# Local attention in tiles of 32 queries and 64 keys, with two heads to a transpose

## The reference

```
WINDOW = 32;  HEADS = 16;  DIM_HEAD = 64;  QK_SCALE = 8
def local_attention(q, k, v):          # b, h, n, d
    # queries in windows of 32; each window sees its own 32 keys and the 32 before
    mask = (it < jb) | (it > jb + w) | (jb == -1)
    sim = einsum('bhwie,bhwje->bhwij', bq, bk2) * QK_SCALE     # 32 x 64 per window
    attn = softmax(where(mask, -max, sim))
    out = einsum('bhwij,bhwje->bhwie', attn, bv2)
def attn_layer(x, Wqkv, qs, ksc, Wo):
    q, k, v = split(x @ Wqkv);  q = l2norm(q) * qs;  k = l2norm(k) * ksc
    q, k = rotary with position scales (q, k)
    return local_attention(q, k, v) @ Wo
for i in range(6):
    x = attn_layer(shift_tokens(x), ...) + x
    x = ffn_layer(shift_tokens(x), ...) + x      # layer norm, 128 -> 2 x 341, a * gelu(gate), -> 128
```

## Time and profile before

| | |
|---|---|
| time, median of 3 runs | 3379.95 us (3378.38 to 3385.42) |
| the profiled execution's own time | 3382.95 us |
| its span | 3380.9 us |
| TensorE matmuls busy | 2973.2 us (88%), 29755 instructions |
| DVE, ACT, POOL busy | 71%, 55%, 38% |
| chain that ended last | TensorE 76%, DVE 16%, everything else 8% |
| DMA | 127.31 MB, 13.1% of 16 engines on the main queue |

### The profile page before, as it was taken

One profiled execution on the slowest core, in us unless ns is written; L12 is line 12 of the kernel. 1 busy time (PEld: TensorE's weight loads), 2 busy tenths in 40 slices (PEclk: granted clock), 3 DMA queues, 4 the chain that ended last, 5 costly groups with the idle time before them and its releaser, 6 DMA issues.

```text
span 3380.9 us, 74255 instructions
## 1 busy us (share of the span) xinstructions
PE 2973.2 (88%) x29755; PEld 1802.7 (53%) x29812; DVE 2400.9 (71%) x3960; ACT 1874.8 (55%) x4990; POOL 1290.9 (38%) x851
## 2 busy tenths in 40 slices
PE   4669858475979799999599999999999999999997
PEld 3544546352334333333376666666666666666665
DVE  4950289537940677776688888888888888888885
ACT  4221331135422266666377777777777777777774
POOL 0010000100000111111377766766776676676663
PEclk7579855597989799999799999999999999999999
DMA  2000000000000100000221212122121221211111
GB/s 100 3 1 0 36 3 3 1 0 0 0 0 0 61 23 23 24 22 16 99 56 48 52 46 79 48 59 73 45 59 49 79 53 45 79 48 47 42 44 40
DMA packets 38966, 127.31 MB, mean 38 GB/s; under 512 B 8480, under 2 KB 10784, under 8 KB 36736
## 3 DMA queue, kind: packets, MB, share of 16 engines
q1 hardware_dynamic: 38656, 122.96, 13.1%
HBM read 43.57 MB, written 5.44 MB: 14 GB/s over the span
## 4 chain that ended last, share of the span: by engine, by line
PE 76%; DVE 16%; DVEq 2%; ACT 2%; issue 2%; DMA 1%; POOLq 1%; ACTq 0%; SPq 0%; POOL 0%
PE ps L1481 15%; PE ps L648 7%; PE ps L1533 6%; PE ps L1523 5%; PE ps L1499 5%; PE ps L1541 5%; PE ps L1514 5%; DVE arena L972 4%; PE ps L1076 4%; PE ps L1104 4%; PE ps L1554 4%; PE ps L1091 3%; PE ps L1506 2%; PE ps L1560 2%; PE ps L200 1%
## 5 line engine op out<-in xcount | busy, mean ns | idle before, releaser
L1481 PE MATMUL ps<-arena 128*128 128x512 f32 x1152 | 555.3, 604 | 15.8 <-ACTq L1763 14.4
L1828 ACT ACTIVATE arena<-ps,arena 128x96 f32<-128x96 f32 x1536 | 497.9, 350 | 81.4 <-DVE arena L2017 81.3
L2094 POOL TENSOR_TENSOR arena<-arena 128x1024 f32<-128x1024 f32 x190 | 448.7, 2362 | 113.5 <-DVE arena L1908 113.5
L2100 POOL TENSOR_TENSOR arena<-arena 128x2048 f32<-128x2048 f32 x95 | 344.2, 3623 | 199.0 <-ACT arena L1770 193.6
L1241 DVE TENSOR_REDUCE arena<-ps 128x1 f32<-128x512 f32 x512 | 329.5, 686 | 77.2 <-PE ps L1076 72.0
L1203 ACT ACTIVATE arena<-ps 128x1024 f32<-128x1024 f32 x256 | 262.2, 1024 | 178.6 <-PE ps L1091 169.9
L2089 POOL TENSOR_TENSOR arena<-arena 128x768 f32<-128x768 f32 x192 | 282.7, 1472 | 131.4 <-DVE arena L1943 131.4
L1828 ACT ACTIVATION_READ_ACCUMULATOR arena<-ps,arena 128x1 f32 x1536 | 332.6, 217 | 0.0
L1903 DVE TENSOR_TENSOR arena<-ps,arena 128x1024 f32<-128x1024 f32 x192 | 235.1, 1225 | 121.4 <-PE ps L1481 107.8
L1481 PEld LDWEIGHTS ps<-arena 128*128 128x128 f32 x1152 | 197.6, 191 | 169.9 <-issue 157.6
L191 POOL TENSOR_SCALAR rstd<-mv 128x4 f32<-128x4 f32 x32 | 8.1, 252 | 718.7 <-DVE mv L178 718.7
(11 more groups left out here) (285 smaller groups left out, 5422.8 us busy)
## 6 DMA issues: line engine op xcount, KB each, us to landing
arena<-pack_l SPq DMA_DIRECT2D x48, 384.0 KB, 4.1
arena<-grow SPq DMA_DIRECT2D x48, 384.0 KB, 4.0
arena<-in_deep SPq DMA_DIRECT2D x6, 2649.5 KB, 9.5
arena<-pack_l SPq DMA_DIRECT2D x48, 256.0 KB, 3.5
arena<-grow SPq DMA_DIRECT2D x48, 256.0 KB, 3.4
arena<-in_rotary SPq DMA_DIRECT2D x6, 1024.0 KB, 8.4
arena<-pack_l SPq DMA_DIRECT2D x48, 128.0 KB, 2.3
pack_tern<-in_tern SPq DMA_DIRECT2D x2, 2888.0 KB, 10.5
```

Source lines behind the costliest of these rows:

```text
L1481: last = T.matmul(m.ps[0:rows.stop - rows.start, at + half, :], f.xs[t % 2][:, rows], w.wqkv[:, j * INNER + half * BLK:j * INNER + (half + ...
L1828: last = A(f.prob[:, p, :], m.ps[:, 4 + j % 2, i * SPAN:(i + 1) * SPAN], ACT.Exp, bias=f.nmax[t % 2][:, p:p + 1], accum_out=f.rsum[t % 2][ ...
L2094: G.tensor_tensor(f.rot[t % 2][:, here], f.rot[t % 2][:, here], f.sin[:, here], ALU.add)
L2100: G.tensor_tensor(r, r, spread(f.ss[t % 2], DH), ALU.mult).then_inc(s["rotated"], 1)
```

## The change

`SPAN`, the keys of a product, goes from 96 to 64, and the queries from 64 to 32 (`WINS` = 4 windows a tile). Scores are computed for each head in 4 products of 32 queries and 64 keys; the bands have 64 columns for each head. Within a call, heads are taken in pairs (even, odd) so that exponentials write the probabilities of head 2k and 2k+1 beside each other. A transpose then takes such a pair, 128 columns, and puts the even head's keys on rows 0 to 63 and the odd head's on rows 64 to 127; `probs(j)` makes 4 of them in one bank, and `pT` is half as wide. Value products take 64 rows and 32 queries, 4 a head. For this the values must lie on the same rows as the probabilities: `vraw` is written with all even heads first and then all odd ones, and the spreading puts even heads on rows 0 to 63 and odd ones on rows 64 to 127, for each window 64 rows: 8 DMAs, and 2 for the next tile's first 32 rows. Since `probs(1)` has a bank of its own now, its wait on the copy of the first half (`p_copied`) goes.

```diff
@@ -40,7 +40,7 @@
...
 PACKS = {
-    "const": [("ident", P), ("band", 96), ("band0", 96), ("cT", 2 * LAYERS)],
+    "const": [("ident", P), ("band", 64), ("band0", 64), ("cT", 2 * LAYERS)],
     "mod": [("wmod", LAYERS * 6 * P)],
@@ -1437,11 +1437,11 @@
...
 WIN = 32
+WINS = P // WIN
 HALF = P // 2
-SPAN = WIN + HALF
+SPAN = 2 * WIN
 KEYS = WIN + P
 FRONT = WIN + 1
-ORDER = [h for half in range(2) for odd in range(2) for h in range(8 * half + odd, 8 * half + 8, 2)]
 GROUP = 4
@@ -1468,7 +1468,7 @@
...
-    return sum(2 + (u % BT != 0) for u in range(t % 2, t + 1, 2))
+    return sum(8 + 2 * (u % BT != 0) for u in range(t % 2, t + 1, 2))
@@ -1507,32 +1507,32 @@
...
         for i in range(GROUP):
-            for half in range(2):
+            for w in range(WINS):
                 for e in range(2):
-                    h = ORDER[GROUP * (j + e) + i]
-                    rows = slice(DH * e, DH * e + DH)
-                    last = T.matmul(m.ps[HALF * half:HALF * (half + 1), 4 + e, i * SPAN:(i + 1) * SPAN],
-                                    f.qT[rows, h // 2, HALF * half:HALF * (half + 1)],
-                                    f.kT[t % 2][rows, h // 2, HALF * half:HALF * half + SPAN], start=False, stop=True,
+                    k = 2 * j + i
+                    rows, queries = slice(DH * e, DH * e + DH), slice(WIN * w, WIN * (w + 1))
+                    last = T.matmul(m.ps[queries, 4 + e, i * SPAN:(i + 1) * SPAN], f.qT[rows, k, queries],
+                                    f.kT[t % 2][rows, k, WIN * w:WIN * w + SPAN], start=False, stop=True,
                                     skip_group_check=True)
-                    if i == GROUP - 1 and half == 1:
+                    if i == GROUP - 1 and w == WINS - 1:
                         last.then_inc(s["scored"], 1)
...
     def probs(j):
-        for i in range(8):
-            last = T.transpose(m.ps[0:SPAN, PROB_AT + i // 4, (i % 4) * P:(i % 4 + 1) * P], f.prob[:, 8 * j + i, :],
-                               m.ident)
+
+        for i in range(GROUP):
+            last = T.transpose(m.ps[:, PROB_AT + j, i * P:(i + 1) * P], f.flat_prob[:, 4 * j + i, :], m.ident)
         last.then_inc(s["p_made"], 1)
...
     def heads(t):
-        for i in range(QB):
-            for half in range(2):
-                col = (i % 4) * P + HALF * half
+        for n in range(QB):
+            for w in range(WINS):
                 for e in range(2):
-                    h = 2 * i + e
-                    last = T.matmul(m.ps[DH * e:DH * (e + 1), HEADS_AT + i // 4, col:col + HALF],
-                                    f.v[t % 2][0:SPAN, half, h * DH:(h + 1) * DH],
-                                    f.pT[0:SPAN, ORDER.index(h), HALF * half:HALF * (half + 1)], start=True, stop=True)
+                    i = (n + 4 * e) % QB
+                    rows, queries = slice(DH * e, DH * (e + 1)), slice(WIN * w, WIN * (w + 1))
+                    col = (i % 4) * P + WIN * w
+                    last = T.matmul(m.ps[rows, HEADS_AT + i // 4, col:col + WIN],
+                                    f.v[t % 2][rows, w, i * DH:(i + 1) * DH], f.pT[rows, i, queries],
+                                    start=True, stop=True)
         last.then_inc(s["heads"], 1)
@@ -1634,7 +1634,6 @@
...
         if behind:
-            pe.wait_ge(s["p_copied"], 2 * t - 1)
             pe.wait_ge(s["normed"], 2 * t)
@@ -1824,7 +1823,7 @@
...
             for i in range(GROUP):
-                p = GROUP * j + i
+                p = 8 * (j // 2) + 2 * i + j % 2
                 last = A(f.prob[:, p, :], m.ps[:, 4 + j % 2, i * SPAN:(i + 1) * SPAN], ACT.Exp,
@@ -1857,8 +1856,7 @@
...
         act.wait_ge(s["p_made"], 2 * t + 1)
-        A(f.pT[0:SPAN, 0:8, :], wide(PROB_AT, SPAN).rearrange("p a (i b) -> p (a i) b", b=P),
-          ACT.Copy).then_inc(s["p_copied"], 1)
+        A(f.pT[:, 0:4, :], m.ps[:, PROB_AT, :].rearrange("p (i b) -> p i b", b=P), ACT.Copy).then_inc(s["p_copied"], 1)
@@ -1880,7 +1878,8 @@
...
     for v in f.v:
-        V.memset(v[0:WIN, 0, :], 0.0)
+        for e in range(2):
+            V.memset(v[DH * e:DH * e + WIN, 0, :], 0.0)
     V.memset(f.mean, 1.0 / P)
@@ -1929,12 +1928,12 @@
...
             dve.wait_ge(s["v_spread"][(t - 1) % 2], 16 * v_moves(t - 1))
-        V.tensor_copy(f.vraw[t % 2].rearrange("p (a b) -> p a b", a=2), m.ps[:, at:at + 2, :]).then_inc(s["v_copied"], 1)
+        V.tensor_copy(f.vraw[t % 2].rearrange("p (e i d) -> p i e d", e=2, d=DH),
+                      m.ps[:, at:at + 2, :].rearrange("p a (i e d) -> p (a i) e d", e=2, d=DH)).then_inc(s["v_copied"], 1)
...
         dve.wait_ge(s["p_made"], 2 * t + 2)
-        V.tensor_copy(f.pT[0:SPAN, 8:16, :],
-                      m.ps[0:SPAN, PROB_AT:PROB_AT + 2, :].rearrange("p a (i b) -> p (a i) b", b=P))\
+        V.tensor_copy(f.pT[:, 4:8, :], m.ps[:, PROB_AT + 1, :].rearrange("p (i b) -> p i b", b=P))\
             .then_inc(s["p_copied"], 1)
@@ -2014,7 +2013,7 @@
...
             dve.wait_ge(s["scored"], 4 * t + j + 1)
-            V.tensor_reduce(f.nmax[t % 2][:, GROUP * j:GROUP * (j + 1)],
+            V.tensor_reduce(f.nmax[t % 2][:, 8 * (j // 2):8 * (j // 2) + 8].rearrange("p (i e) -> p e i", e=2)[:, j % 2, :],
                             m.ps[:, 4 + j % 2, 0:GROUP * SPAN].rearrange("p (h k) -> p h k", h=GROUP), AX, ALU.max,
@@ -2174,12 +2173,18 @@
...
         sp.wait_ge(s["v_copied"], t + 1)
-        sp.dma_start(v[t % 2][WIN:SPAN, 0, :], raw[0:HALF, :]).then_inc(s["v_spread"][t % 2], 16)
-        sp.dma_start(v[t % 2][0:SPAN, 1, :], raw[WIN:P, :]).then_inc(s["v_spread"][t % 2], 16)
+        for e in range(2):
+            here, at = slice(e * BLK, (e + 1) * BLK), DH * e
+            sp.dma_start(v[t % 2][at + WIN:at + SPAN, 0, :], raw[0:WIN, here]).then_inc(s["v_spread"][t % 2], 16)
+            for w in range(1, WINS):
+                sp.dma_start(v[t % 2][at:at + SPAN, w, :], raw[WIN * (w - 1):WIN * (w + 1), here])\
+                    .then_inc(s["v_spread"][t % 2], 16)
         if t % BT != BT - 1:
...
                 sp.wait_ge(s["heads"], t)
-            sp.dma_start(v[(t + 1) % 2][0:WIN, 0, :], raw[P - WIN:P, :]).then_inc(s["v_spread"][(t + 1) % 2], 16)
+            for e in range(2):
+                sp.dma_start(v[(t + 1) % 2][DH * e:DH * e + WIN, 0, :], raw[P - WIN:P, e * BLK:(e + 1) * BLK])\
+                    .then_inc(s["v_spread"][(t + 1) % 2], 16)
@@ -2226,9 +2231,10 @@
...
     f.sin = a.take(2 * INNER)
-    f.v = [a.take(2 * INNER).rearrange("p (a b) -> p a b", a=2) for _ in range(2)]
-    f.pT = a.take(LH * P).rearrange("p (a b) -> p a b", b=P)
-    f.prob = a.take(LH * SPAN).rearrange("p (a b) -> p a b", b=SPAN)
+    f.v = [a.take(2 * INNER).rearrange("p (a b) -> p a b", a=WINS) for _ in range(2)]
+    f.pT = a.take(QB * P).rearrange("p (a b) -> p a b", b=P)
+    prob = a.take(LH * SPAN)
+    f.prob, f.flat_prob = (prob.rearrange("p (a b) -> p a b", b=n) for n in (SPAN, 2 * SPAN))
     f.kT = [a.take(QB * KEYS).rearrange("p (a b) -> p a b", b=KEYS) for _ in range(2)]
@@ -2464,9 +2470,9 @@
...
-    i, j = np.arange(P)[:, None], np.arange(96)[None, :] - 32
-    seen = (j <= i % 64) & (j >= i % 64 - 32)
-    first = seen & ((j >= 0) | (i >= 64))
+    i, j = np.arange(P)[:, None], np.arange(2 * WIN)[None, :] - WIN
+    seen = (j <= i % WIN) & (j >= i % WIN - WIN)
+    first = seen & ((j >= 0) | (i >= WIN))
     big = np.float32(-1e30)
...

```

## The result

The changed kernel takes 3456.65 us (median of 4 runs, 3453.61 to 3458.89) against 3380.44 before: a ratio of 1.0223, 95% interval 1.0211 to 1.0236. It is slower by 76 us, 2.2%; forecast were 51 us, 1.5%. The profiled execution took 3453.61 us, its span is 3451.7.

The account below looks back on a forecast made before the run. TensorE was taken to bound the last stage; value products +1.88, scores -0.26, transposes -0.88 and bands -0.21 gave +0.53 us a visit, times 96 +51 us: 3431 us, range 3382 to 3480.

Parts of the forecast that it names:

- What bounds the kernel: Last stage, 96 visits: its time is the sum of TensorE's blocks, busy 1666.88 of 1676 us at full clock.
- The value products: Heads block: 64 rounds, each as long as loading 64 stationary columns; 3.90 us against 2.02, +1.88 us a visit.
- Rival A: Value products: the load hides, a round is 32 ns, heads costs only +0.16 us a visit; 3266 us, chance 0.12.
- Rival B: Scores and value products: each instruction costs its start, +2.58 us a visit; 3628 us, chance 0.04.
- The scores: Score blocks, two calls a visit: middle taken between -0.21 and -0.05 us a call, -0.13; -0.26 us a visit.
- the ideal of 8 rounds: Score block: eight products at once, limited by streaming; 0.61 us against 0.82, -0.21 us a call.
- Transposes and bands: Transposes of probabilities, 4 a call instead of 8: -0.88 us a visit; bands, 256 columns instead of 384: -0.21.
- What lies beside: Shorter DVE, ACT and POOL work, and spreading the values in 10 DMAs instead of 3: no gain and no cost.
- The sum: All terms together: +0.53 us a visit, times 96 visits, +51 us; 3431 us, 1.5% slower.
- DVE keeps up: Condition in e1's forecast of 3281 us: DVE, 13.3 us busy a visit of 15.9, does not delay TensorE.
- the 3.5 us in the expectations: Expectation for e5: an instruction fetch takes about 3.5 us until usable; 128 pairs running in less must wait.

Follow-up runs that it names:

- e2: Changed kernel with only 32 of each head's 64 value features stationary in the value products; 3367.18 us, ratio to before 0.9961.
- e3: Changed kernel with 64 moving query columns instead of 32 in each value product; 3455.12 us, ratio to before 1.0218.
- e1: Changed kernel with head h paired with h+8 for the transposes, so value products use all four array quarters; 3354.79 us, ratio to before 0.9912.
- e8: Changed kernel with each of the 8 main spreading DMAs cut in two, 18 issues a visit instead of 10; 3462.95 us, ratio to before 1.0243.
- e5: e1 with the key projection moved in front of the second group's scores; 3310.10 us, ratio to before 0.9796.
- e7: e1 with values of windows 2 and 3 not spread, 4 main DMAs a tile instead of 8; 3342.86 us, ratio to before 0.9887.

## Why the prediction was right, and where a size was off

**What bounds the kernel.** Right: before and after, the stage is the sum of TensorE's blocks at full clock. The differences of the blocks add up to the 76 us by which the stage grew.

**The value products.** Right in mechanism and size: forecast 3.90 us a block, measured 3.85. That a round lasts as long as the load of its 64 stationary columns was read from durations of loads and from one slow row elsewhere; e2 and e3 now show it in place, from both sides, and e1 shows that each quarter has its own load: four at once give 2.00 us. The single starts say the same. In the changed kernel they come in pairs, 6 to 7 ns apart, a pair every 58 ns; in e3, with twice the moving columns, also every 58; in e2, with half the stationary ones, every 32; in e1 they come in fours, every 58. Rival A (3266 us), the load that hides, did not happen. Rival B (3628 us), a price for each instruction, falls with e1: 128 instructions in 2.00 us are 16 ns each. The rule of the Trainium skill's page "TensorE: Matmul & The Clock Gate", section "Wait — 56ns, not 53.3ns?", that starts never come closer than about 25 ns, does not hold here; the scores' 64 starts in 0.65 us show the contrary, at a granted clock of 1.00.

**The scores.** The step that failed in size: "I take the middle, -0.13" a call; it measured -0.03 in the chain, and -0.016 as the mean of the stage's 191 blocks. The earlier trace rows had the answer without any middle: 64 starts in 0.64 us. After, in the scores' line alone (stretch, us, busy and started, clock):

```profile
2498.56:2498.80 0.24, 0.23 (x31) 1.00 0.00 0
2498.56:2499.21 0.65, 0.64 (x64) 1.00 0.00 0
```

These are the rows of the other stage almost to the hundredth, at twice the clock. I had kept the ideal of 8 rounds as one end, though the nearest row showed the pace that the block then had. The row's value, 0.64 + 0.134 = 0.77 a call, would have given -0.10 a visit instead of -0.26, a sum of +0.69, +66 us. That is 15 of the 22 us by which this term was off; the rest is that the blocks gained still less than the row said.

**Transposes and bands.** Right: -82.0 of -84 us, -20.3 of -20. One reading was off without effect: 0.42 ns a column is the shorter bands' block (0.32 us for 768 columns), and not the most, as the longer one gives 0.56; both blocks became 0.10 us shorter.

**What lies beside.** Right: the spreading is hidden, and e8 shows that even 18 issues a visit leave the stage as long as it was. The wide blocks' +6 us had no term in the sum. 4.6 of them lie in the query projection, from its first start to that of the value products behind it (1.87 us instead of 1.82, 93 times); the cause was not tried.

**The sum.** +51 forecast, +76 measured in the stage: 22 us are the scores, 6 the wide blocks and 2 the transposes, less 4 in the value products and 1 in the rest.

**Why e1 gained less than its blocks.** Of the forecast of e1, the step "DVE keeps up" was not what failed. The pauses come at multiples of about 127 load-and-product pairs (381, 253, 634 or 1267 apart), and the page of the changed kernel counts 311 packets of instructions on queue 8, 16384 bytes each, where that of before has 221. These 90 more go with 11520 more products and as many loads on TensorE: 23040 instructions, 256 a packet, 64 bytes each. So a packet holds 128 pairs. In the changed kernel no 128 pairs run in under 2.9 us, and no pause is over 0.5 us; in e1 some run in 2.0 us, and pauses of 1 to 2 us follow. Putting 1.72 us of wide matmuls between took the scores' pauses away (e5).

The times of the packets in e1's trace settle it. In the pause shown above a packet on queue 8 starts at 2508.55 us and has landed at 2510.03; TensorE goes on at 2511.37, 1.34 us later. Of the 54 pauses over 0.5 us between 1700 and 3300 us, 52 end 1.2 to 1.65 us after such a landing; only 7% of all moments of that stretch lie so behind one. From a packet's start to TensorE's restart it is 2.2 to 3.2 us, 2.5 in the middle. So TensorE waited for its instructions, and the 3.5 us in the expectations, an estimate from e1's pauses, were too long. In e7, with half of the main moves, the same distance is 2.5 us as well, so a disturbance of the fetch by other DMAs is not shown.

## What to carry to other kernels

For small f32 matmuls like these count rounds, not instructions or columns: a round on the tiles in use lasted as long as the longer of streaming and loading (58 ns with 64 stationary columns, 32 ns with 32 and 32), so cutting the moving side below the stationary side bought nothing, and spreading operands so that all four quarters have work bought half the block. When a block of small matmuls becomes quick, look at instruction supply: after the first 32 pairs they came at 10 to 12 ns each, and where 128 pairs ran in about 2 us, TensorE stopped for 1 to 2 us, until wide matmuls stood in between. Take the value of the nearest measured row, not the middle between it and an ideal.

## What the runs showed of the hardware that was not expected

- TensorE stopped for up to 1.9 us with no engine or DMA of the program behind it (e1: 49.0 us in the scores' blocks, 45 times), where 128 load-and-product pairs ran in about 2 us; 52 of 54 pauses ended 1.2 to 1.65 us after a 16384-byte packet of instructions had landed.
- Such pauses can cost more than themselves: in e1's profiled execution the granted clock was 0.50 for nine stretches of 3.4 us, each at most 1.4 us behind the end of a pause of 1.3 to 1.9 us.
- The pace of starts in a block of 64 small products is the same at both clocks: 64 in 0.64 us at 0.50 and in 0.65 at 1.00.
- In value products that are bound by the load, twice the moving columns cost 0.03 us in 3.85 (e3).
